# Attention of an eight-core transformer layer: half the row-sum matmuls, one VectorE addition instead, and the block's closing step placed inside the next block

## The chip, the cores and the metric

The kernel runs on all 8 cores of one Trainium2 chip (trn2). The cores form two dies (cores 0 to 3 and 4 to 7). The metric is the device time of one execution in microseconds (us), taken on the slowest core. Every core runs the same program on its own data; the cores exchange nothing.

## What is computed

One layer on x of shape (2, 4096, 4096) in float32. The core of the reference:

```python
xn = _layernorm(x, axis=-1)
x = x + attn(xn, w_qkv, w_o) + ffn(xn, gate, kernel, bias, lora_A, lora_B, ...)

# attn
qkv = einsum('bsd,od->bso', xn, w_qkv)      # 32 query heads, 8 key/value heads of 128
q, k = rope(q), rope(k)
scores = einsum('bhqd,bhkd->bhqk', q, k) / sqrt(128), causal mask
out = einsum('bhqk,bhkd->bhqd', softmax(scores), v)
return einsum('bso,do->bsd', out, w_o)

# ffn: one dense layer with bias and two low-rank terms
xn @ kernel + bias + B_eff (A_eff xn) + B_shared (A_shared xn)
```

Here batch is 2 and the sequence 4096, so four query heads share one key/value head, and each query position attends to itself and what is before it.

## The kernel before, in words

Each core owns 1024 of the 8192 tokens: two chunks of 512 (`CH`) of one batch, an early one (query block `qb` 0) and a late one (`qb` 1). It runs stages one after another, with a barrier between most: layer norm of the whole batch's 4096 tokens together with the K projection, the V projection (both `kp` on TensorE), the Q projection (`q_p`), the low-rank inputs (`lp_`), the attention (`a_`), the output projection (`w_p`), and the dense layer with the final sum (`f_p`). Weights and intermediate tensors (`sc_q`, `sc_k`, `sc_v`, `sc_xkv`) go through the chip's memory.

Nothing schedules the work but the code: `call` (L76) and `dma` (L103) append to one plan per engine, in the order in which the Python runs, and each engine executes its plan in that order. `wait` (L51) puts a wait on a semaphore in the plan of the engine that calls it; one counter per engine (`s_pe`, `s_ve`, `s_ac`) counts finished instructions. All TensorE matmuls that count up have the line L81, all others L86; all GpSimd loads have L111. `gd` is the GpSimd (POOL) queue, which issues the attention's loads.

The attention is `attention()` (L622). It runs over 8 key/value heads, 2 duos of query heads and 2 query blocks: 32 **blocks**, each for two heads `z` = 0 and 1. A block has 4 **visits** to chunks of 512 keys for `qb` 0 and 8 for `qb` 1 (`VISITS`, L26), 192 in all. The last visit of a block is the diagonal one (`DIAG`). A visit has two halves `g` of 256 keys, and a half has two key tiles `t` of 128. With two heads and two halves there are four probability tiles `a_p` (`psb`, index `2*z+g`).

`scores(z, g, ...)` (L663) makes two matmuls of K tile by Q into the two halves of `a_s`, one exponential of 128x1024 on ScalarE into `a_p`, and in the diagonal visit two products with the mask `p_cm` on VectorE. `avrows(z, g, ...)` (L693) makes, for each of the two key tiles, the value product (V tile by probabilities, into `a_av`) and the **row sum** (a weight of one column of ones, `p_onesb`, by the same probabilities, into the first partition of `a_rw`). These four matmuls alternate. They are accumulated in PSUM over the whole block.

The order within a visit is written out by hand (L744 to L756): scores of half 0 for both heads, `avrows` of half 1 of the visit before, scores of half 1, `avrows` of half 0. A score needs `a_s` of its head to be free (`scdep`, set by the exponential).

When the block's last `avrows` are done, the block is closed for each head (L761 to L782): the reciprocal of the row sum on VectorE (`a_rc`, 1x512), a matmul with a row of ones that spreads it over 128 partitions into `a_rw` (`p_onesf`; float32, it runs as two matmul instructions), a copy to `a_bc`, and the product of `a_av` and `a_bc` into `p_attn`. `a_rc`, `a_bc` and each head's Q tile exist once. The next block's loads (Q, then K and V of its first visit) are issued when the block's last reader is done (`qdep`, L727); K and V of the later visits go into three buffers each, one visit ahead (`load_kv`, L650).

After the attention the first output weights (`w_w`, 4 MB) are issued on the GpSimd queue (L786), and a barrier stands before the projection (L788).

## Time and profile before

| What | Value |
|---|---|
| Median of the runs before | 5046.68 us (2 runs: 4911.06 and 5182.3) |
| The profiled execution, its own time | 4911.6 us |
| Its span on the slowest core (core 6) | 4910.1 us |
| Spans of the 8 cores | 4871.8 to 4910.1 us, mean granted clock 0.901 to 0.905 |
| TensorE (PE) busy over the span | 4035.2 us, 82% |
| VectorE (DVE) busy | 1112.6 us, 23% |
| ScalarE (ACT) busy | 974.5 us, 20% |
| GpSimd (POOL) busy | 534.0 us, 11% |

The page is of one execution on its slowest core. PE is TensorE's matmuls, PEld its weight loads, which can overlap matmuls. Matmuls are pipelined: one is longer than the distance to the next, so the distance between the starts tells the rate. Where rows give the idle time before an instruction, the name behind the arrow is what ended it; "issue" is time in which the engine waited for nothing that the profile shows. PEclk is the TensorE clock that was granted, as a share of 2.4 GHz: 0.50 is the lower of the two levels, 1.2 GHz.

### The profile page before, as it was taken

Reading aid. Unit: us, or ns where it says so; the run is one execution under the profiler, and the core shown is the slowest. Engines: PE = TensorE matmul, PEld = TensorE weight load, DVE = VectorE, ACT = ScalarE, POOL = GpSimd, SP = SyncE. Lnnn points to the kernel's source line nnn. Section 1 sums busy time; section 2 is a strip of 40 time slices with the busy share of each in tenths; the row PEclk is TensorE's granted clock in tenths of the full one; section 3 lists DMA queues with packets and bytes.
Section 4 is the critical chain, followed back from the end, with each engine's and each line's share of the span. In section 5 each row is a group of like instructions: output and inputs, shape, how many; then the busy total and the mean of one; then the engine's idle time right before and its main releaser. Section 6 shows DMA issues by size and latency. Waiting matters only on the chain.

```text
span 4910.1 us, 44374 instructions; the slowest of 8 cores (4871.8 to 4910.1 us)
## 1 busy us (share of the span) xinstructions
PE 4035.2 (82%) x15827; PEld 1522.3 (31%) x16144; DVE 1112.6 (23%) x1874; ACT 974.5 (20%) x1041; POOL 534.0 (11%) x828
## 2 busy tenths in 40 slices
PE   3788786499939994888888888888888999568999
PEld 0333232144414441322222222222222444223334
DVE  0544454011002221122222222222222101012222
ACT  3112210000000000144444444444444000000000
POOL 1000000000000000122222222222221000000000
PEclk7899898799969997988988888888888999889999
DMA  9744622633156666011111111111113554466763
GB/s 139 140 95 86 117 79 63 131 99 111 54 113 90 102 87 133 19 36 35 35 33 37 32 33 36 34 35 35 33 36 62 101 106 88 98 140 138 143 135 97
DMA packets 398741, 394.61 MB, mean 80 GB/s; under 512 B 61888, under 2 KB 359104, under 8 KB 398400
## 3 DMA queue, kind: packets, MB, share of 16 engines
q0 software_dynamic: 214752, 223.94, 27.1%
q1 hardware_dynamic: 183776, 167.82, 11.4%
q8 instruction: 136, 2.23, 0.2%
q14 instruction: 77, 0.63, 0.0%
HBM read 470.30 MB, written 83.89 MB: 113 GB/s over the span
## 4 chain that ended last, share of the span: by engine, by line
PE 69%; DVE 10%; DMA 7%; another core or an unknown queue 7%; ACT 3%; issue 3%; SPq 0%; DVEq 0%; POOL 0%; ACTq 0%; POOLq 0%
PE kp L86 16%; PE a_rw L81 12%; PE w_p L86 9%; PE q_p L86 9%; PE a_av L86 8%; DMA f_at<-sc_at 5%; DVE a_rc L81 4%; PE a_s L86 4%; PE a_s L81 4%; PE f_p L86 4%; DVE f_s L81 2%; ACT a_p L81 1%; ACT lkv_q L81 1%; PE lp_pl L86 1%
## 5 line engine op out<-in xcount | busy, mean ns | idle before, releaser
L81 ACT ACTIVATE a_p<-a_s,p_btab 128x1024 bf16<-128x1024 f32 x768 | 814.0, 1111 | 2197.0 <-PE a_s L81 2197.0
L81 PE MATMUL a_rw<-a_p,p_onesb 128*1 128x512 bf16 x1536 | 581.4, 379 | 14.3 <-issue 7.7
L86 PE MATMUL a_av<-a_p,a_v 128*128 128x512 bf16 x1475 | 576.6, 391 | 0.0
L86 PE MATMUL f_p<-f_k,f_x 128*128 128x512 bf16 x2007 | 460.5, 385 | 126.8 <-DMA f_x<-sc_xkv 90.3
L86 PE MATMUL kp<-kv_w,kv_x 128*128 128x512 bf16 x1943 | 437.8, 380 | 92.0 <-DMA kv_w<-wvT 90.0
L86 PE MATMUL kp<-lkv_x,kv_w 128*128 128x512 bf16 x1985 | 462.9, 394 | 50.7 <-DVE kscr L81 21.9
L86 PE MATMUL q_p<-q_x,q_w 128*128 128x512 bf16 x1943 | 438.3, 381 | 78.9 <-DMA q_x<-sc_xkv 76.9
L86 PE MATMUL w_p<-w_w,p_attn 128*128 128x512 bf16 x1943 | 438.4, 381 | 4.3 <-SPq L182 2.3
L81 DVE TENSOR_TENSOR a_p<-a_p,p_cm 128x512 bf16<-128x512 bf16 x256 | 97.4, 422 | 1171.0 <-ACT a_p L81 1171.0
L81 PE MATMUL a_s<-a_q,a_k 128*128 128x512 bf16 x768 | 323.3, 421 | 16.4 <-DMA a_v<-sc_v 9.3
L86 PE MATMUL a_s<-a_q,a_k 128*128 128x512 bf16 x734 | 308.1, 420 | 14.1 <-ACT a_p L81 14.1
L81 PE MATMUL a_rw<-a_rc,p_onesf 1*128 1x512 f32 x128 | 124.4, 1070 | 236.7 <-DVE a_rc L81 236.7
L86 PEld LDWEIGHTS f_p<-f_k,f_x 128*128 128x128 bf16 x2048 | 198.1, 99 | 374.1 <-issue 154.2
L86 PEld LDWEIGHTS kp<-lkv_x,kv_w 128*128 128x128 bf16 x2032 | 204.1, 101 | 312.7 <-issue 100.3
L86 PEld LDWEIGHTS kp<-kv_w,kv_x 128*128 128x128 bf16 x1984 | 194.6, 98 | 325.8 <-issue 93.2
L86 PEld LDWEIGHTS q_p<-q_x,q_w 128*128 128x128 bf16 x1984 | 194.7, 98 | 313.2 <-issue 80.9
L111 POOL DMA_DIRECT2D a_k<-sc_k x384 | 200.8, 525 | 792.8 <-PE a_s L81 754.8
L86 PEld LDWEIGHTS w_p<-w_w,p_attn 128*128 128x128 bf16 x1984 | 194.7, 98 | 239.7 <-issue 7.4
L81 PEld LDWEIGHTS a_rw<-a_p,p_onesb 128*1 128x1 bf16 x1536 | 121.7, 79 | 428.3 <-issue 428.3
L86 PEld LDWEIGHTS a_av<-a_p,a_v 128*128 128x128 bf16 x1536 | 149.5, 97 | 318.3 <-issue 280.4
L81 ACT ACTIVATE lkv_q<-lkv_x 128x512 bf16<-128x512 bf16 x256 | 149.7, 623 | 485.1 <-PE lkv_pq L81 420.9
L81 DVE CAST kscr<-kp 128x512 bf16<-128x512 f32 x128 | 84.1, 688 | 693.7 <-PE kp L81 656.1
(90 smaller groups left out, 2085.1 us busy)
## 6 DMA issues: line engine op xcount, KB each, us to landing
lkv_x<-xTkv POOLq DMA_DIRECT2D x32, 1024.0 KB, 27.3
sc_xkv<-lkv_x SPq DMA_DIRECT2D x128, 256.0 KB, 4.0
kv_x<-sc_xkv SPq DMA_DIRECT2D x8, 4096.0 KB, 15.5
q_w<-wqT POOLq DMA_DIRECT2D x16, 2048.0 KB, 17.4
w_w<-woT POOLq DMA_DIRECT2D x8, 4096.0 KB, 26.5
f_k<-kern POOLq DMA_DIRECT2D x8, 4096.0 KB, 32.6
a_k<-sc_k POOLq DMA_DIRECT2D x384, 64.0 KB, 2.1
a_v<-sc_v POOLq DMA_DIRECT2D x192, 128.0 KB, 2.8
```

Source lines behind the costliest of these rows:

```text
L81: getattr(eng, m)(*aa, **kk).then_inc(s, st)
L86: getattr(eng, m)(*aa, **kk)
L111: eng.dma_start(**kk).then_inc(s, 16)
```

## The change

Three things change, all in `attention()`.

- In `scores`, VectorE adds the two key tiles of the probabilities (after the mask, where there is one) into a new bf16 tile `prow` (`a_w`, four of them), and `avrows` makes one row-sum matmul from it instead of two from `a_p`. The two value products now come first, then the row sum, which waits for the addition.
- The loops over heads, duos, query blocks and visits become one list of 192 visits (`sched`). K and V of a block's first visit are loaded during the visit before, the Q tiles are doubled (`qpar`) and loaded then too (`load_q`), and the three K and V buffers turn with the running number of the visit.
- The closing of a block (`finalize`) is placed in the next block's first visit, after its four scores and ahead of its first value products; the last `avrows` of the old block stand between the new block's first two and second two scores. `a_rc` and `a_bc` exist once per head.

```diff
             psb = [p2(nc.sbuf_tensor(f"a_p{i}", [128, 2 * CH], BF16)) for i in range(4)]
-            rcs = p2(nc.sbuf_tensor("a_rc", [1, CH], F32))
-            bcs = p2(nc.sbuf_tensor("a_bc", [128, CH], F32))
+            prow = [p2(nc.sbuf_tensor(f"a_w{i}", [128, CH], BF16)) for i in range(4)]
+            rcs = [p2(nc.sbuf_tensor(f"a_rc{i}", [1, CH], F32)) for i in range(2)]
+            bcs = [p2(nc.sbuf_tensor(f"a_bc{i}", [128, CH], F32)) for i in range(2)]
...
+            def load_q(bi):
+                kvh, duo, qb = blocks[bi]
+                qpar = bi % 2
+                qh = (4 * kvh + 2 * duo, 4 * kvh + 2 * duo + 1)
+                for z in range(2):
+                    h = qh[z]
+                    gd.wait(s_pe, qdep.get((z, qpar), 0))
+                    qld[(z, qpar)] = [
+                        gd.dma(out=qsb[z][0:64, qpar * CH:(qpar + 1) * CH],
...
                     exv[(z, g)] = mv
                     exk[(z, g)] = "ve"
+                    ve.wait(s_ve, mv)
                 else:
                     exv[(z, g)] = a
                     exk[(z, g)] = "ac"
+                    ve.wait(s_ac, a)
+                ve.wait(s_pe, prdep[zz])
+                pav = ve.call("tensor_add", prow[zz][:],
+                              psb[zz][:, 0:CH], psb[zz][:, CH:2 * CH])
+                exv[(z, g, "row")] = pav
...
                             psb[zz][:, t * CH:(t + 1) * CH],
                             start=(first and t == 0), stop=(last and t == 1),
                             inc=False)
-                    pe.call("matmul", p_rw[z][0:1, :], sb_onesb[:, 0:1],
-                            psb[zz][:, t * CH:(t + 1) * CH],
-                            start=(first and t == 0), stop=(last and t == 1))
+                pe.wait(s_ve, exv[(z, g, "row")])
+                pe.call("matmul", p_rw[z][0:1, :], sb_onesb[:, 0:1],
+                        prow[zz][:], start=first, stop=last)
                 pbdep[zz] = pe.ctr.v
...
+            load_q(0)
+            kvst[0] = load_kv(blocks[0][0], VISITS[sched[0][2]][1], 0)
+            for gi, (bi, vi, v) in enumerate(sched):
+                qpar = bi % 2
+                par = gi % 3
+                kl, vl = kvst[gi]
+                if gi + 1 < NG:
+                    nbi, nvi, nv_ = sched[gi + 1]
+                    kvst[gi + 1] = load_kv(blocks[nbi][0], VISITS[nv_][1],
+                                           (gi + 1) % 3)
+                    if nvi == 0:
+                        load_q(nbi)
+                scores(0, 0, v, par, qpar, kl)
+                scores(1, 0, v, par, qpar, kl)
+                if gi > 0:
+                    pvl = kvst[gi - 1][1]
+                    ppar = (gi - 1) % 3
+                    avrows(0, 1, ppar, pvl, False, vi == 0)
+                    avrows(1, 1, ppar, pvl, False, vi == 0)
+                scores(0, 1, v, par, qpar, kl)
+                scores(1, 1, v, par, qpar, kl)
+                if vi == 0 and bi > 0:
+                    finalize(bi - 1)
+                avrows(0, 0, par, vl, vi == 0, False)
+                avrows(1, 0, par, vl, vi == 0, False)
```

`finalize(bi)` holds the closing step of before, word for word but for the indices of `a_rc` and `a_bc`.

TensorE, one half visit inside a block, before. In the names, a_s is the scores, a_q and a_k the Q and K tiles, a_p the probabilities (0 and 1 are head 0, 2 and 3 head 1), a_v the V tile; the number behind a_s, a_av and a_rw is the head.

```order
L86 MATMUL a_s0<-a_q0,a_k1 128x512
L81 MATMUL a_s0<-a_q0,a_k1 128x512
L86 MATMUL a_s1<-a_q1,a_k1 128x512
L81 MATMUL a_s1<-a_q1,a_k1 128x512
L86 MATMUL a_av0<-a_p0,a_v1 128x512
L81 MATMUL a_rw0<-a_p0,p_onesb 1x512
L86 MATMUL a_av0<-a_p0,a_v1 128x512
L81 MATMUL a_rw0<-a_p0,p_onesb 1x512
L86 MATMUL a_av1<-a_p2,a_v1 128x512
L81 MATMUL a_rw1<-a_p2,p_onesb 1x512
L86 MATMUL a_av1<-a_p2,a_v1 128x512
L81 MATMUL a_rw1<-a_p2,p_onesb 1x512
```

The same half of a visit after the change (of the visit that uses the third K and V buffers); a_w is the sum of the two key tiles of a_p.

```order
L86 MATMUL a_s0<-a_q0,a_k2 128x512
L81 MATMUL a_s0<-a_q0,a_k2 128x512
L86 MATMUL a_s1<-a_q1,a_k2 128x512
L81 MATMUL a_s1<-a_q1,a_k2 128x512
L86 MATMUL a_av0<-a_p0,a_v2 128x512 x2
L81 MATMUL a_rw0<-a_w0,p_onesb 1x512
L86 MATMUL a_av1<-a_p2,a_v2 128x512 x2
L81 MATMUL a_rw1<-a_w2,p_onesb 1x512
```

Two of the four row sums are gone, and the value products of one head stand next to each other.

TensorE at the end of a block, before: the last `avrows`, the two broadcasts (a_rw from a_rc), and the next block's scores.

```order
L86 MATMUL a_av1<-a_p3,a_v0 128x512
L81 MATMUL a_rw1<-a_p3,p_onesb 1x512
L86 MATMUL a_av1<-a_p3,a_v0 128x512
L81 MATMUL a_rw1<-a_p3,p_onesb 1x512
L81 MATMUL a_rw0<-a_rc,p_onesf 128x512
L81 MATMUL a_rw1<-a_rc,p_onesf 128x512
L86 MATMUL a_s0<-a_q0,a_k0 128x512
L81 MATMUL a_s0<-a_q0,a_k0 128x512
L86 MATMUL a_s1<-a_q1,a_k0 128x512
L81 MATMUL a_s1<-a_q1,a_k0 128x512
L86 MATMUL a_s0<-a_q0,a_k0 128x512
```

The same place after.

```order
L86 MATMUL a_av0<-a_p1,a_v0 128x512 x2
L81 MATMUL a_rw0<-a_w1,p_onesb 1x512
L86 MATMUL a_av1<-a_p3,a_v0 128x512 x2
L81 MATMUL a_rw1<-a_w3,p_onesb 1x512
L86 MATMUL a_s0<-a_q0,a_k1 128x512
L81 MATMUL a_s0<-a_q0,a_k1 128x512
L86 MATMUL a_s1<-a_q1,a_k1 128x512
L81 MATMUL a_s1<-a_q1,a_k1 128x512
L81 MATMUL a_rw0<-a_rc0,p_onesf 128x512
L81 MATMUL a_rw1<-a_rc1,p_onesf 128x512
L86 MATMUL a_av0<-a_p0,a_v1 128x512 x2
L81 MATMUL a_rw0<-a_w0,p_onesb 1x512
```

The two broadcasts moved behind the four score pairs of the next block's first visit; the new block's value products stand behind them.

VectorE at the end of a block, before: mask products of the diagonal visit, the closing of heads 0 and 1, then the next block's first mask product.

```order
L81 TENSOR_TENSOR a_p1<-a_p1,p_cm4 128x512 x2
L81 TENSOR_TENSOR a_p3<-a_p3,p_cm4 128x512 x2
L81 RECIPROCAL a_rc<-a_rw0 1x512
L81 COPY a_bc<-a_rw0 128x512
L81 TENSOR_TENSOR p_attn<-a_av0,a_bc 128x512
L81 RECIPROCAL a_rc<-a_rw1 1x512
L81 COPY a_bc<-a_rw1 128x512
L81 TENSOR_TENSOR p_attn<-a_av1,a_bc 128x512
L81 TENSOR_TENSOR a_p0<-a_p0,p_cm4 128x512 x2
```

And after: the last addition of the diagonal visit (behind its mask product), the four additions of the new block's first visit, then the closing.

```order
L81 TENSOR_TENSOR a_w3<-a_p3 128x512
L81 TENSOR_TENSOR a_w0<-a_p0 128x512
L81 TENSOR_TENSOR a_w2<-a_p2 128x512
L81 TENSOR_TENSOR a_w1<-a_p1 128x512
L81 TENSOR_TENSOR a_w3<-a_p3 128x512
L81 RECIPROCAL a_rc0<-a_rw0 1x512
L81 COPY a_bc0<-a_rw0 128x512
L81 TENSOR_TENSOR p_attn<-a_av0,a_bc0 128x512
L81 RECIPROCAL a_rc1<-a_rw1 1x512
L81 COPY a_bc1<-a_rw1 128x512
L81 TENSOR_TENSOR p_attn<-a_av1,a_bc1 128x512
L81 TENSOR_TENSOR a_w0<-a_p0 128x512
```

The first reciprocal moved behind the additions for all four exponentials of the new block's first visit.

## Rows read from the trace of the kernel before

**Rows 1.** Busy time by stretch (times each), PEclk, DMA share, GB/s; core 6.

```profile
core 6: us, PE busy (x) PEld busy (x) DVE busy (x) ACT busy (x) POOL busy (x), PEclk, DMA share, GB/s
2053.00:3800.00 1747.00, 1472.39 (x4641) 422.50 (x4734) 397.09 (x448) 813.96 (x768) 409.76 (x694) 0.88 0.13 36
...
3840.00:4200.00 360.00, 358.26 (x1636) 163.23 (x1668) 35.97 (x52) 0.00 (x0) 10.05 (x6) 1.00 0.49 90
```

**Rows 2.** Chain that ended last, within 2053 to 3800 us, by line.

```profile
by line: PE a_rw L81 32.6%; PE a_av L86 23.5%; DVE a_rc L81 12.1%; PE a_s L86 12.0%; PE a_s L81 10.3%; ACT a_p L81 3.6%; issue 3.0%; DVE a_bc L81 1.3%; DVE p_attn L81 1.3%; DVEq L60 0.2%; ACTq L60 0.0%; PE w_p L86 0.0%; SPq L60 0.0%; SPq L1
```

**Rows 3.** Timeline, one half visit: start, length (us), engine, line, instruction, [idle before].

```profile
2613.05 0.39 PE L86 MATMUL a_s<-a_q,a_k 128*128 128x512 bf16 x1
2613.28 0.38 PE L81 MATMUL a_s<-a_q,a_k 128*128 128x512 bf16 x1
...
2613.76 2.12 ACT L81 ACTIVATE a_p<-a_s,p_btab 128x1024 bf16<-128x1024 f32 x2 [1.26 <-PE a_s L81]
2613.93 0.38 PE L86 MATMUL a_av<-a_p,a_v 128*128 128x512 bf16 x1
2614.23 0.08 PEld L81 LDWEIGHTS a_rw<-a_p,p_onesb 128*1 128x1 bf16 x1 [0.42 <-issue]
2614.24 0.38 PE L81 MATMUL a_rw<-a_p,p_onesb 128*1 128x512 bf16 x1
...
2614.55 0.39 PE L86 MATMUL a_av<-a_p,a_v 128*128 128x512 bf16 x1
...
2616.43 0.39 PE L86 MATMUL a_s<-a_q,a_k 128*128 128x512 bf16 x1
```

**Rows 4.** Timeline at the end of a block (2624 to 2642 us).

```profile
2624.62 3.35 DVE L81 RECIPROCAL a_rc<-a_rw 1x512 f32<-1x512 f32 x1 [1.13 <-PE a_rw L81]
...
2625.40 0.38 PE L81 MATMUL a_rw<-a_p,p_onesb 128*1 128x512 bf16 x1
...
2628.12 2.04 PE L81 MATMUL a_rw<-a_rc,p_onesf 1*128 1x512 f32 x2 [2.34 <-DVE a_rc L81]
...
2630.33 0.69 DVE L81 COPY a_bc<-a_rw 128x512 f32<-128x512 f32 x1 [2.36 <-PE a_rw L81]
...
2631.13 0.69 DVE L81 TENSOR_TENSOR p_attn<-a_av,a_bc 128x512 bf16<-128x512 f32 x1
...
2631.74 3.33 DVE L81 RECIPROCAL a_rc<-a_rw 1x512 f32<-1x512 f32 x1
...
2635.22 2.04 PE L81 MATMUL a_rw<-a_rc,p_onesf 1*128 1x512 f32 x2 [5.06 <-DVE a_rc L81]
2637.19 0.61 PE L86 MATMUL a_s<-a_q,a_k 128*128 128x512 bf16 x1
...
2637.59 0.63 PE L81 MATMUL a_s<-a_q,a_k 128*128 128x512 bf16 x1
2638.01 0.63 PE L86 MATMUL a_s<-a_q,a_k 128*128 128x512 bf16 x1
...
2638.32 2.12 ACT L81 ACTIVATE a_p<-a_s,p_btab 128x1024 bf16<-128x1024 f32 x2 [15.68 <-PE a_s L81]
...
2639.58 0.58 PE L86 MATMUL a_s<-a_q,a_k 128*128 128x512 bf16 x1 [0.50 <-ACT a_p L81]
...
2641.78 0.38 PE L81 MATMUL a_rw<-a_p,p_onesb 128*1 128x512 bf16 x1
```

**Rows 5.** Chain of waits, two of head 0's reciprocals: start, length, what.

```profile
2583.45 3.36 DVE a_rc L81
...
2692.73 3.36 DVE a_rc L81
```

**Rows 6.** Busy time by stretch, at a block end.

```profile
2587.00:2600.00 13.00, 7.44 (x12) 1.75 (x13) 6.02 (x5) 2.61 (x3) 4.66 (x8) 0.50 0.22 64
```

**Rows 7.** Groups of the page: busy us, mean ns, idle before.

```profile
L81 PE MATMUL a_rw<-a_p,p_onesb 128*1 128x512 bf16 x1536 | 581.4, 379 | 14.3 <-issue 7.7
L81 DVE TENSOR_TENSOR a_p<-a_p,p_cm 128x512 bf16<-128x512 bf16 x256 | 97.4, 422 | 1171.0 <-ACT a_p L81 1171.0
```

**Rows 8.** Timeline, the diagonal visit's exponentials and mask products.

```profile
2617.14 2.12 ACT L81 ACTIVATE a_p<-a_s,p_btab 128x1024 bf16<-128x1024 f32 x2 [1.26 <-PE a_s L81]
...
2618.35 0.76 DVE L81 TENSOR_TENSOR a_p<-a_p,p_cm 128x512 bf16<-128x512 bf16 x2 [20.61 <-ACT a_p L81]
```

**Rows 9.** Timeline, the first output weights and projection; landing time from the page's DMA issues.

```profile
w_w<-woT POOLq DMA_DIRECT2D x8, 4096.0 KB, 26.5
...
3770.95 1.72 POOL L111 DMA_DIRECT2D w_w<-woT  x1 [1.78 <-issue]
...
3799.93 2.29 PE L86 MATMUL w_p<-w_w,p_attn 128*128 128x512 bf16 x5 [2.29 <-SPq L182]
```

More of the change, by code:

```diff
@@ L627, in attention @@
                 ve.waitd(cmld)
-                qsb = [p2(nc.sbuf_tensor(f"a_q{i}", [128, CH], BF16)) for i in range(2)]
+                qsb = [p2(nc.sbuf_tensor(f"a_q{i}", [128, 2 * CH], BF16)) for i in range(2)]
                 kb = [p2(nc.sbuf_tensor(f"a_k{i}", [128, CH], BF16)) for i in range(3)]
@@ L636, in attention @@
                 p_rw = [p2(nc.psum_tensor(f"a_rw{i}", [128, CH], F32)) for i in range(2)]
-                qdep = [0, 0]
+                blocks = [(kvh, duo, qb)
+                          for kvh in range(KVH) for duo in range(2) for qb in range(2)]
+                sched = []
+                for bi, (kvh, duo, qb) in enumerate(blocks):
+                    vis = [v for v in range(12) if VISITS[v][0] == qb]
+                    for vi, v in enumerate(vis):
+                        sched.append((bi, vi, v))
+                NG = len(sched)
+                qdep = {}
+                qld = {}
                 kdep = [0, 0, 0]
@@ L642, in attention @@
                 pbdep = [0, 0, 0, 0]
+                prdep = [0, 0, 0, 0]
                 exv = {}
@@ L646, in attention @@
                 rwdep = [0, 0]
-                rcs_dep = 0
-                bcs_dep = 0
+                rcsd = [0, 0]
+                bcsd = [0, 0]
+                kvst = {}
                 def load_kv(kvh, pos, par):
@@ L670, in scores @@
                                 kb[par][:, (2 * g + t) * 128:(2 * g + t + 1) * 128],
-                                qsb[z][:], start=True, stop=True, inc=(t == 1))
+                                qsb[z][:, qpar * CH:(qpar + 1) * CH],
+                                start=True, stop=True, inc=(t == 1))
                     spv = pe.ctr.v
+                    qdep[(z, qpar)] = spv
                     ac.wait(s_pe, spv)
@@ new lines, in finalize @@
+                def finalize(bi):
+                    kvh, duo, qb = blocks[bi]
+                    qh = (4 * kvh + 2 * duo, 4 * kvh + 2 * duo + 1)
+                    for z in range(2):
+                        h = qh[z]
+                        ve.wait(s_pe, pbdep[2 * z])
+                        ve.wait(s_pe, pbdep[2 * z + 1])
+                        ve.wait(s_pe, rcsd[z])
+                        rv = ve.call("reciprocal", rcs[z][0:1, :], p_rw[z][0:1, :])
+                        rwdep[z] = rv
+                        pe.wait(s_ve, rv)
+                        bv = pe.call("matmul", p_rw[z][:, :], sb_onesf[0:1, :],
+                                     rcs[z][0:1, :], start=True, stop=True)
+                        rcsd[z] = bv
+                        ve.wait(s_pe, bv)
+                        ve.wait(s_ve, bcsd[z])
+                        cv = ve.call("tensor_copy", bcs[z][:], p_rw[z][:, :])
+                        rwdep[z] = cv
+                        ve.wait(s_ve, cv)
+                        nv2 = ve.call("tensor_mul",
+                                      sb_attn[:, h * TOWN + qb * CH:
+                                              h * TOWN + (qb + 1) * CH],
+                                      p_av[z][:], bcs[z][:])
+                        avdep[z] = nv2
+                        bcsd[z] = nv2
@@ L784, in build_program @@
+                gl = NG - 1
+                avrows(0, 1, gl % 3, kvst[gl][1], False, True)
+                avrows(1, 1, gl % 3, kvst[gl][1], False, True)
+                finalize(len(blocks) - 1)
         attention()
```

78 lines of the change are left out of this document (10 added, 68 removed).

## The prediction

> **What bounds the kernel now.** I first took the two wide stretches that have the attention's matmul shapes and the output projection's [rows 1]. In the attention (2053 to 3800 us) TensorE is busy for 1472 of 1747 us, ScalarE for 814, VectorE for 397 and GpSimd for 410, at a mean granted clock of 0.88; in the projection the clock is 1.00, and 1636 matmuls take 358 us, 0.22 us each. So the attention belongs to TensorE, and what it loses there it loses to something other than a busy neighbour. The chain of waits inside the attention says to what [rows 2]: TensorE's row sums (a_rw) hold 32.6% of it, the value products (a_av) 23.5%, the scores (a_s) 22.3%, and VectorE's reciprocal (a_rc) 12.1%. Those are two different things, a stream of matmuls and a stall at block ends, so I read one of each in the timeline.
>
> The stream [rows 3]: four score matmuls start 0.22 us apart (the first value product starts 0.88 after the first of them); from there value products and row sums alternate, 0.31 us apart (2613.93, 2614.24, 2614.55). Eight of these and the four scores are half a visit, 2613.05 to 2616.43: 3.38 us, of which ScalarE's two exponentials take 2.12. The row sum's weight load (one column) starts only as its own matmul does, not under the matmul before. The score pairs write alternate halves of a tile as well and still start 0.22 apart, so what costs 0.09 is, as I read it, the switch between 128-column and 1-column weights.
>
> The block end [rows 4]: the last row sum starts at 2625.40, the next block's first score at 2637.19. Between them lies one chain, for each head: reciprocal 3.35, broadcast matmul pair 2.04, copy 0.69, product 0.69; head 1's reciprocal waits in VectorE's queue for all of head 0's. From the first reciprocal's start (2624.62) to the first score it is 12.57 us. The same reciprocal of the next long and short blocks together comes at 2583.45 and 2692.73 [rows 5]: 109.28 us for 24 half visits, which by 3.38 are 81.1; 28.2 are left, **14.1 us lost per block end**. Of those 11.5 are the gap and the rest the restart at half clock: the granted clock is 0.50 from 2587 to 2600 [rows 6], scores start 0.43 apart, and head 0's next pair waits for its exponential until 2639.58; row sums are back at 0.31 from 2641.78, 6.6 us after the second broadcast began [rows 4]. Check: 16 such pairs of blocks are 1748 us, the length of the attention.
>
> **The change, part by part.** (1) Row sums. There are 1536 of them, 379 ns long each [rows 7]; half go. Each pair of value products now runs back to back and one row sum follows. Value product to value product I cost at 0.22, the pitch of equal-width neighbours in [rows 1, 3]; then 0.31 and 0.31 for the two switches: 0.84 where there were 1.25. A half visit becomes 0.88 + 2 x 0.84 = **2.56 us**, 0.82 less; 192 visits have 384 halves: **-315 us**. The unseen pitch lies between 0.22 and 0.31; at 0.31 a half visit is 2.74 and the part brings 246. Below: 330, if rounding is in our favour.
>
> The Trainium skill (TensorE: Matmul & The Clock Gate, Step-by-step: what each phase is for) says that the array's queue pulls the next weights ahead of the running matmul, so that neighbours are spaced by the moving columns alone. By that, a removed row sum is worth 0.22, not 0.41. The trace agrees for equal widths and contradicts it where widths alternate.
>
> (2) Does something else end later than 2.56? ScalarE: the exponentials start 0.71 after the first score, the second ends at 2.83, and a score that waits for one starts 0.15 after its end (2638.32 + 1.11 to 2639.58) [rows 3, 4]: head 1's next score may go at 2.98 and is due at 2.56 + 0.44 = 3.00. It just fits; there is no more to gain from TensorE here without ScalarE becoming the bound. VectorE: 768 new additions of 128x512 bf16. The nearest row is the mask product, 0.38 us apart and 0.42 long, started 0.10 after its exponential [rows 8]; ends are 0.38 and the 0.69 of the PSUM copy [rows 4]. They are off the path: in a plain half visit head 1's sum is ready at 2.83 + 0.10 + 0.42 = 3.35, and its row sum is due at 2.56 + 0.88 + 0.84 + 0.44 = 4.72. In the diagonal visit VectorE has 2 x (0.76 + 0.42) plus gaps, 2.5 of 2.56 us, and is ready at about 4.5; it fits. At 0.69 each it would be 0.4 late in 64 half visits, +25 us. The added waits sit in VectorE's queue, behind which only the next sums stand.
>
> (3) Loads. The new block's first K, V and Q are issued a visit ahead, not after the last row sum. This removes nothing: TensorE waited for the reciprocals, not for them. 0 us; GpSimd's work does not grow.
>
> (4) Block end. This is where the text of the change and the order part. The four first exponentials of the next block are done before the stall, but TensorE still takes its instructions in order: after the scores of half visit 0 and 1 stand both broadcasts, so it waits for **both reciprocals** before any value product. And VectorE reaches the first reciprocal only after the additions for those last scores. Let T be the start of the new block's third score pair. Exponentials end at T+2.83, addition at +2.93, reciprocal at +3.31; the chain of 12.57 is unchanged, so the first value product starts at T+15.88. TensorE's own work ended at T+0.88: **15.0 us of gap against 11.5**. The restart: the second broadcast begins at T+13.91, so full clock by the same 6.6 us at T+20.5. Head 0's three matmuls run at half clock (0.5 lost), head 1's value product waits for its accumulator's last reader (13.91 + 2.21 + 0.80 + 0.69 + 0.10 = T+17.7, 0.45 lost), then 2.8 us at half clock lose 1.4. Together 17.4, **3.3 more than 14.1**; 31 block ends of 32 move (the last stays): **+102 us**. Ends: 16.4 (no wait, prompt clock) is +71; 19 is +152.
>
> (5) After the attention. The first output weights are issued at 3770.95 and land 26.5 later; the projection starts at 3799.93 [rows 9]. Five half visits less 0.82 bring the end 4.1 closer: 24.9 are left, so about 2 us show. Bounds 0 and 5.
>
> Sum against the profiled execution (4911.6 us, its span 4910.1 on the slowest core): 4911.6 - 315 + 102 + 2 = **4701 us**, -4.3%. The median before is 5046.68, of two runs at 4911.06 and 5182.3; the profile goes with the lower, and so does my forecast. 
>
> **Rivals.**
> - *A row sum is worth only its columns* (0.22, case W): the switch costs nothing by itself and another cause keeps the 0.31 for the rest. 384 x 2 x 0.22 = 169; 4911.6 - 169 + 104 = 4847. For it: no row shows two value products in a row. Against: scores at 0.22.
> - *The block end is hidden, as the new order suggests* (case H): if TensorE did not stand still, 14.1 would fall to about 4 (broadcasts): 4911.6 - 315 + 2 - 31 x 10.1 = 4286. Against: the broadcasts stand in line ahead of the value products, and nothing after them can pass.
> - *The clock thins* (case P): were the denser stream granted 0.81 instead of 1.00, each of ten matmuls would cost 0.05 more, 384 x 0.5 = 192: 4893. Against: the projection, denser still, has 1.00 [rows 1]. The Trainium skill (same page, Seeing it yourself) has a peak-current limit of 13/16 when three cores of a die run dense matmuls; this trace, with eight, does not show it.
> - *The clock does not come back* (case C, the slow side): after a gap of 15 us, cut by two broadcasts, the clock stays at its lower level well into the block. A half visit at the low level costs 10 x 0.21 = 2.1 us more. The gain of 211 is gone at 100 such half visits; through all short blocks (some 107 beyond the restart) it is 4926; slower by over 2% from 147 on; in the whole stage 5421. For it: the stage has 0.88 now. Against: it comes back 6.6 us after the broadcast, at every block end I read, and no stall is left inside a block.
>
> **How the numbers follow.** Forecast 0.81, W 0.10, P 0.03, H 0.02, C 0.04 (three quarters of it slower by over 2%). The likeliest's own ends: low 4911.6 - 330 + 71 = 4653; high 4911.6 - 246 + 152 + 25 + 5 = 4848 with all of it bad together. W ends there too. I take 4640 to 4840; what lies above is most of P and C, below is H. Faster by over 2% (under 4813): the forecast, H and the lower edge of W, 0.84. Within 2%: the rest of W, P, a quarter of C, 0.13. Slower: 0.03.
>
> **What would show it.** Timeline: half visits 2.5 to 2.6 us apart, with value product to value product at 0.22 (if 0.31, part 1 is wrong by 70 us). Row sums 768 in number. From the last score of a new block's first visit to its first value product 15 us, with the first reciprocal starting 3.3 us after the third score pair; TensorE's waits for a_rc 31 x (5.8 + 5.1) and the last pair, some 345 us in all (237 now: 64 x 3.7). Consecutive same-head reciprocals of a long and a short block: 24 x 2.56 + 2 x 17.4 = 96.2 us apart in place of 109.3. Attention near 1535 us long. If that distance is under 85, the block end was hidden; if TensorE's idle before a_av names VectorE in mid-block, the additions are late; a granted clock under 0.8 in the stretch speaks for C.

## The result, and the profile after

The changed kernel takes 4713.77 us (median of 11 runs, lowest 4697.02); against the kernel before the ratio is 0.9579, with a 95% interval of 0.9554 to 0.9603: 4.2% faster. The chip has executions in which a die runs at a lower clock, before and after alike; the ratio is of the undisturbed ones, and the kernel before has a median of 5139.74 with them and of about 4914 without. The profiled execution has a span of 4713.8 us on the slowest core, core 3.

The forecast was 4701 against a profiled execution of 4911.6, a ratio of 0.957. As a share of that execution it came out; the parts don't all hold, and the places are named further down. To compare stages across runs I use the length of the attention, from the start of the first exponential to the start of the last product into p_attn: 1745.6 us before (2053.0 to 3798.6), 1527.9 after (2049.4 to 3577.3).

The stretch of the attention after the change, columns as in [rows 1]:

```profile
core 3: us, PE busy (x) PEld busy (x) DVE busy (x) ACT busy (x) POOL busy (x), PEclk, DMA share, GB/s
...
2515.00:2529.00 14.00, 3.68 (x4) 0.99 (x4) 8.74 (x6) 1.33 (x2) 0.99 (x2) 0.55 0.06 19
...
2534.00:2552.00 18.00, 17.92 (x71) 5.11 (x69) 8.80 (x22) 14.79 (x15) 7.76 (x14) 1.00 0.21 61
2049.00:3577.00 1528.00, 1172.77 (x3967) 320.78 (x3965) 711.83 (x1215) 813.99 (x768) 410.56 (x696) 0.83 0.15 41
```

TensorE has 300 us less work, ScalarE and GpSimd have the same, VectorE 315 more. Within a block TensorE is as full as before (17.92 of 18 us; 17.85 of 18 before, from 2600 to 2618); what grew is the share of time at the block ends, so the mean granted clock fell from 0.88 to 0.83.

One half visit, from the timeline; it answers to [rows 3]:

```profile
2503.18 0.39 PE L86 MATMUL a_s<-a_q,a_k 128*128 128x512 bf16 x1
...
2503.88 2.12 ACT L81 ACTIVATE a_p<-a_s,p_btab 128x1024 bf16<-128x1024 f32 x2 [0.43 <-PE a_s L81]
2504.05 0.59 PE L86 MATMUL a_av<-a_p,a_v 128*128 128x512 bf16 x2
2504.58 0.38 PE L81 MATMUL a_rw<-a_w,p_onesb 128*1 128x512 bf16 x1
2504.89 0.60 PE L86 MATMUL a_av<-a_p,a_v 128*128 128x512 bf16 x2
2505.16 0.42 DVE L81 TENSOR_TENSOR a_w<-a_p 128x512 bf16<-128x512 bf16 x1 [1.12 <-ACT a_p L81]
...
2505.73 0.39 PE L86 MATMUL a_s<-a_q,a_k 128*128 128x512 bf16 x1
```

2503.18 to 2505.73 are 2.55 us in place of 3.38. Two value products in a row are 0.59 long together, so their starts are 0.22 apart; where the widths change, starts are still 0.31 apart.

A block end, answering to [rows 4]; T, the start of the new block's third score pair, is 2513.51:

```profile
2513.51 0.39 PE L86 MATMUL a_s<-a_q,a_k 128*128 128x512 bf16 x1
...
2514.17 0.38 PE L81 MATMUL a_s<-a_q,a_k 128*128 128x512 bf16 x1
...
2516.51 0.42 DVE L81 TENSOR_TENSOR a_w<-a_p 128x512 bf16<-128x512 bf16 x1 [0.58 <-ACT a_p L81]
2516.85 3.34 DVE L81 RECIPROCAL a_rc<-a_rw 1x512 f32<-1x512 f32 x1
2520.33 2.04 PE L81 MATMUL a_rw<-a_rc,p_onesf 1*128 1x512 f32 x2 [5.78 <-DVE a_rc L81]
...
2523.88 3.33 DVE L81 RECIPROCAL a_rc<-a_rw 1x512 f32<-1x512 f32 x1
2527.36 2.04 PE L81 MATMUL a_rw<-a_rc,p_onesf 1*128 1x512 f32 x2 [4.99 <-DVE a_rc L81]
2529.34 1.03 PE L86 MATMUL a_av<-a_p,a_v 128*128 128x512 bf16 x2
...
2531.14 1.01 PE L86 MATMUL a_av<-a_p,a_v 128*128 128x512 bf16 x2 [0.26 <-DVE p_attn L81]
```

The reader sees the reciprocal right behind the last addition (T+3.34), the value product at T+15.83, and the gap, 2514.39 to 2529.34, of 15.0 us. The same reciprocal of a long and a short block together comes at:

```profile
2267.69 3.27 DVE a_rc L81
...
2363.44 3.27 DVE a_rc L81
```

95.75 us for what took 109.28 [rows 5]; 24 half visits are 61.3, so a block end loses 17.2. TensorE's longest waits in 2040 to 3600 us (who waited for whom: us, times, longest):

```profile
PE a_rw L81 <- DVE a_rc L81: 342.6, 64, 5.8
...
PE w_p L86 <- DMA w_w<-woT: 12.3, 1, 12.3
...
PE a_av L86 <- DVE p_attn L81: 8.0, 31, 0.3
```

No addition (a_w) is among them. Two are new: 0.3 us at each block end for head 0's or head 1's product, which the prediction had in its sum, and 12.3 us for the projection's first weights, where [rows 9] had only the barrier.

What stands behind the attention grew too. From the start of the last product into p_attn to the end of the span it is 1111.5 us before and 1136.5 after, on the slowest core of each: 10.1 more until the projection starts, 6.1 more of waiting for the dense layer's first input (before, then after), and 10.1 more in the dense layer itself (569.9 and 580.0 us), less 1.2 in the projection. The mean over the eight cores is 14.5 more, 9.1 of it in the dense layer.

```profile
PE f_p L86 <- DMA f_x<-sc_xkv: 90.3, 1, 90.3
PE f_p L86 <- DMA f_x<-sc_xkv: 96.4, 1, 96.4
```

### The profile page after: what moved, and what is told of

Read it like the earlier page. It is cut to its first block, busy times and chain, and to the rows that moved or that the text cites. A ratio compares the mean times of both kernels' runs of the same rounds, so it can differ in the third digit from the quotient of the medians.

```text
span 4713.8 us, 46036 instructions; the slowest of 8 cores (4661.6 to 4713.8 us)
## 1 busy us (share of the span) xinstructions
PE 3745.1 (79%) x15376; PEld 1419.8 (30%) x15376; DVE 1427.8 (30%) x2642; ACT 974.0 (21%) x1041; POOL 534.3 (11%) x828
## 4 chain that ended last, share of the span: by engine, by line
PE 70%; DVE 10%; DMA 8%; another core or an unknown queue 7%; ACT 3%; issue 2%; SPq 0%; DVEq 0%; POOL 0%; ACTq 0%; POOLq 0%
PE kp L86 19%; PE q_p L86 9%; PE w_p L86 9%; PE a_av L86 8%; PE a_rw L81 7%; PE f_p L86 5%; DMA f_at<-sc_at 5%; PE a_s L86 4%; DVE a_rc L81 4%; PE a_s L81 3%; DVE f_s L81 1%; DMA lkv_x<-xTkv 1%; ACT lkv_q L81 1%; PE lp_pl L86 1%
## 5 line engine op out<-in xcount | busy, mean ns | idle before, releaser
L86 PE MATMUL f_p<-f_k,f_x 128*128 128x512 bf16 x2048 | 471.1, 390 | 133.0 <-DMA f_x<-sc_xkv 96.4
L81 DVE TENSOR_TENSOR a_w<-a_p 128x512 bf16<-128x512 bf16 x768 | 326.5, 425 | 638.8 <-ACT a_p L81 561.0
L86 PE MATMUL kp<-kv_w,kv_x 128*128 128x512 bf16 x1984 | 440.7, 380 | 89.9 <-DMA kv_w<-wvT 89.9
L86 PE MATMUL q_p<-q_x,q_w 128*128 128x512 bf16 x1984 | 440.9, 380 | 80.9 <-DMA q_x<-sc_xkv 80.9
L86 PE MATMUL kp<-lkv_x,kv_w 128*128 128x512 bf16 x2032 | 461.9, 391 | 47.1 <-DVE lkv_x L81 25.2
L86 PE MATMUL a_av<-a_p,a_v 128*128 128x512 bf16 x1536 | 487.2, 400 | 8.5 <-DVE p_attn L81 8.0
L86 PE MATMUL w_p<-w_w,p_attn 128*128 128x512 bf16 x1984 | 440.1, 380 | 12.3 <-DMA w_w<-woT 12.3
L81 PE MATMUL a_rw<-a_rc,p_onesf 1*128 1x512 f32 x128 | 130.4, 1119 | 342.6 <-DVE a_rc L81 342.6
L86 PEld LDWEIGHTS f_p<-f_k,f_x 128*128 128x128 bf16 x2048 | 199.7, 100 | 388.7 <-issue 172.4
L86 PE MATMUL a_s<-a_q,a_k 128*128 128x512 bf16 x768 | 304.6, 397 | 13.4 <-DMA a_k<-sc_k 9.9
L81 PE MATMUL a_rw<-a_w,p_onesb 128*1 128x512 bf16 x768 | 302.6, 394 | 0.0
L81 PE MATMUL a_s<-a_q,a_k 128*128 128x512 bf16 x768 | 299.5, 390 | 0.0
L86 PEld LDWEIGHTS kp<-lkv_x,kv_w 128*128 128x128 bf16 x2032 | 202.7, 100 | 309.6 <-issue 85.9
L86 PEld LDWEIGHTS kp<-kv_w,kv_x 128*128 128x128 bf16 x1984 | 194.5, 98 | 325.7 <-issue 93.1
L86 PEld LDWEIGHTS q_p<-q_x,q_w 128*128 128x128 bf16 x1984 | 194.6, 98 | 317.0 <-issue 84.4
L86 PEld LDWEIGHTS w_p<-w_w,p_attn 128*128 128x128 bf16 x1984 | 194.4, 98 | 248.8 <-issue 15.8
L81 DVE RECIPROCAL a_rc<-a_rw 1x512 f32<-1x512 f32 x64 | 213.6, 3337 | 0.0
L81 DVE TENSOR_TENSOR f_s<-f_p,f_at 128x512 f32<-128x512 f32 x64 | 44.3, 692 | 531.9 <-DMA f_at<-sc_at 317.7
```

The lines of the kernel that those rows point to most:

```text
L81: getattr(eng, m)(*aa, **kk).then_inc(s, st)
L86: getattr(eng, m)(*aa, **kk)
```

## Experiments: the parts alone

**Closing back at its old place.** The row sums, additions and early loads of the change stay:

```diff
-                    if gi > 0:
+                    if vi > 0:
...
-                    if vi == 0 and bi > 0:
-                        finalize(bi - 1)
                     avrows(0, 0, par, vl, vi == 0, False)
                     avrows(1, 0, par, vl, vi == 0, False)
+                    if gi + 1 == NG or sched[gi + 1][1] == 0:
+                        avrows(0, 1, par, vl, False, True)
+                        avrows(1, 1, par, vl, False, True)
+                        finalize(bi)
```

> The changed kernel with one part undone: a block is closed behind its own last row sums again, before the next block's scores; additions, halved row sums and early loads stay. Theory (the rows bring all, the new place of the closing costs 3.3 us at each of 31 block ends): 4911.6 - 315 + 2 = 4599, about 0.936 of the kernel before and 110 less than the changed kernel; half visits 2.56, gap at the block end 11.5 us. Rival (the new place or the overlap of scores and closing brings part of the gain): at or above the changed kernel's 4714.

Measured: lowest 4625.94, ratio 0.9386 (0.9331 to 0.9440) to the kernel before; attention 1447.7 us (2041.6 to 3489.3), **80 less than with the whole change**. TensorE's wait for the reciprocals is 252.4 us, not 342.6. So the new place costs, as expected (ratio 0.9386, where 0.936 was worked out; in us it lies 27 above the 4599, 17 of them in the attention); the size is 2.6 us per block end and not 3.3, because the old place also lost something when visits got shorter. From this run's timeline, the last value products of a block:

```profile
2332.05 0.59 PE L86 MATMUL a_av<-a_p,a_v 128*128 128x512 bf16 x2 [0.20 <-DVE a_p L81]
...
2333.44 0.59 PE L86 MATMUL a_av<-a_p,a_v 128*128 128x512 bf16 x2 [0.41 <-DVE a_p L81]
```

Without the next block's scores between them, the diagonal visit's products wait for the mask (0.2 and 0.4 us), which the change hides.

**Only the row sums**, in the kernel before, with its loads:

```diff
+                    ve.wait(s_pe, prdep[zz])
+                    pav = ve.call("tensor_add", prow[zz][:],
+                                  psb[zz][:, 0:CH], psb[zz][:, CH:2 * CH])
+                    exv[(z, g, "row")] = pav
...
+                    pe.wait(s_ve, exv[(z, g, "row")])
+                    pe.call("matmul", p_rw[z][0:1, :], sb_onesb[:, 0:1],
+                            prow[zz][:], start=first, stop=last)
```

> The kernel before with only the row sums changed (addition on VectorE, one row sum for two); loads and closing as before. Theory (early loads bring nothing): 4599 like the run before it, within 15 us. Rival (the loads at a block's start were hidden only by luck, and with shorter visits they end last): 20 us and more above it, with TensorE waiting for a_k or a_v at block starts.

Measured: lowest 4631.75, ratio 0.9400 (0.9324 to 0.9477); attention 1447.9 us (2049.0 to 3496.9) against 1447.7 with early loads. The early loads bring nothing here. The time is not within 15 us of 4599, as expected, but like the run before it, within 6 us.

**Only the closing's place and the loads**, row sums as before:

```diff
-                    pav = ve.call("tensor_add", prow[zz][:],
-                                  psb[zz][:, 0:CH], psb[zz][:, CH:2 * CH])
...
-                    pe.call("matmul", p_rw[z][0:1, :], sb_onesb[:, 0:1],
-                            prow[zz][:], start=first, stop=last)
+                        pe.call("matmul", p_rw[z][0:1, :], sb_onesb[:, 0:1],
+                                psb[zz][:, t * CH:(t + 1) * CH],
+                                start=(first and t == 0), stop=(last and t == 1))
```

> The changed kernel with its row sums undone: two from the probabilities, no additions; the closing and the loads stay at their new places. Half visits 3.38. Without additions in VectorE's queue the first reciprocal starts 1.2 us before the new block's third score pair, so the gap is 10.5 and not 15.0 us and a block end loses 12.9 in place of 14.1: 4911.6 - 31 x 1.2 = 4875. Rival (the new place costs by itself, through the scores that stand ahead of it or a later clock): 4911.6 + 102 = 5014.

Measured: lowest 4849.55, ratio 0.9842 (0.9766 to 0.9918); attention 1667.7 us (2053.2 to 3720.9), 78 less than before. The direction is the theory's: **alone, the new place is a gain, if one of under 2%; it is a loss together with the additions**. The gain is twice what I expected. The timeline of a block end of this run says why:

```profile
2394.51 0.38 PE L81 MATMUL a_rw<-a_p,p_onesb 128*1 128x512 bf16 x1
...
2394.99 3.35 DVE L81 RECIPROCAL a_rc<-a_rw 1x512 f32<-1x512 f32 x1 [1.99 <-PE a_rw L81]
...
2398.49 1.09 PE L81 MATMUL a_rw<-a_rc,p_onesf 1*128 1x512 f32 x2 [1.37 <-DVE a_rc L81]
...
2404.57 2.04 PE L81 MATMUL a_rw<-a_rc,p_onesf 1*128 1x512 f32 x2 [4.99 <-DVE a_rc L81]
2406.55 0.61 PE L86 MATMUL a_av<-a_p,a_v 128*128 128x512 bf16 x1
```

The first broadcast comes while the clock is still up (granted 1.00 from 2395 to 2399, 0.53 in the ten us behind) and takes 1.09 us, not 2.04; the gap is 9.6 us, not 10.5. So it is at 31 of 32 block ends (1.09 to 1.15). In the kernel before, on its slowest core, 7 of 32 had it at the upper clock already, so some 24 x 0.95 = 23 us come on top of the 37. The other 18 were not traced to a cause; part of them is in the restart, which varies: here matmuls are at full pace from 2409.7 on, 5.1 us after the second broadcast began, over all block ends 6.5 in the mean, and 6.9 in the kernel before.

**One reciprocal ahead of the additions**, the whole change otherwise:

```diff
                         avrows(1, 1, ppar, pvl, False, vi == 0)
+                    if vi == 0 and bi > 0:
+                        recip0()
                     scores(0, 1, v, par, qpar, kl)
```

> The changed kernel with one instruction per block end moved on VectorE: head 0's reciprocal stands ahead of the additions for the new block's third and fourth exponential, not behind them. Theory: it starts at T+0.8 and not T+3.3 (T: start of the third score pair), everything behind it 2.5 us earlier, 31 x 2.5 = 79: 4635. Rival (TensorE's place in the row, not VectorE's queue, sets the gap): no change, 4714.

Measured: lowest 4607.07, ratio 0.9349 (0.9298 to 0.9400); attention 1424.1 us (2054.1 to 3478.2), 104 less than with the change; the time is 28 us under the 4635 expected, mostly by the clock, as follows. The timeline has the reciprocal at 2347.14, T+0.78 (T is 2346.36), the first broadcast again at the upper clock, and the gap at 11.5 us:

```profile
2345.20 0.38 PE L81 MATMUL a_rw<-a_w,p_onesb 128*1 128x512 bf16 x1
...
2347.14 3.34 DVE L81 RECIPROCAL a_rc<-a_rw 1x512 f32<-1x512 f32 x1
...
2350.63 1.09 PE L81 MATMUL a_rw<-a_rc,p_onesf 1*128 1x512 f32 x2 [3.23 <-DVE a_rc L81]
...
2358.68 1.03 PE L86 MATMUL a_av<-a_p,a_v 128*128 128x512 bf16 x2
```

The rival, that TensorE's place in the row alone sets the gap, falls: nothing was changed on TensorE. 2.56 us per block end come from the queue, 79 in all; 0.95 come from the broadcast's clock, at 19 block ends of 32 (at 11 it takes 2.04 us here too), some 18. That is 97 of the 104.

This is not yet all that VectorE's queue costs. Head 0's last row sum starts at 2345.20, and in the kernel with the closing alone the reciprocal started 0.48 us after that row sum (2394.51 to 2394.99). Here it starts 1.94 after it, because the addition for the new block's second exponential still stands ahead of it. By these rows, 1.46 us are left per block end, an estimate of 45 us that no run took back.

## Experiments: what a half visit is bound by

**Both heads' value products first**: two switches of width instead of four.

```diff
+                def avpair(g, par, vl, first, last):
+                    for z in range(2):
...
+                        for t in range(2):
+                            kt = 2 * g + t
+                            pe.call("matmul", p_av[z][:],
...
+                    for z in range(2):
+                        zz = 2 * z + g
+                        pe.wait(s_ve, exv[(z, g, "row")])
+                        pe.call("matmul", p_rw[z][0:1, :], sb_onesb[:, 0:1],
+                                prow[zz][:], start=first, stop=last)
```

> The changed kernel with the four value products of both heads in a row, then both row sums: two switches of weight width in a half visit, not four. By switches alone TensorE would need 0.88 + 3 x 0.22 + 0.31 + 0.22 + 0.31 = 2.38 us. Theory (ScalarE's two exponentials and the way back to the score hold a half visit at 2.54): 2.54, 384 x 0.02, 4706. Rival (ScalarE has room): 2.38, 384 x 0.17 = 65 us less, 4649.

Measured: lowest 4699.94, ratio 0.9549 (0.9520 to 0.9578); attention 1526.8 us (2044.1 to 3570.9) against 1527.9. The total is as expected, but not for the reason that I gave. Half visits are not 2.54: inside a block they alternate between 2.36 and 2.52, 2.44 in the mean.

```profile
2476.74 0.39 PE L86 MATMUL a_s<-a_q,a_k 128*128 128x512 bf16 x1
...
2479.09 0.39 PE L86 MATMUL a_s<-a_q,a_k 128*128 128x512 bf16 x1
...
2479.70 0.38 PE L86 MATMUL a_s<-a_q,a_k 128*128 128x512 bf16 x1
...
2481.61 0.39 PE L86 MATMUL a_s<-a_q,a_k 128*128 128x512 bf16 x1
```

In the longer ones, head 1's scores start 0.61 behind head 0's and not 0.44; that is where ScalarE shows. The half visits gain some 30 us in all, and the block ends give them back: in the mean, the half visit that holds the closing takes 19.55 us in place of 19.11, and the one behind it 3.55 in place of 3.02, 31 x 0.97 = 30. TensorE's waits for the product into p_attn grew from 8.0 to 24.7 us, since head 1's value products now stand right behind head 0's.

**The same with half the exponential.** It leaves out the exponential of the second key tile of each half, whose probabilities stay zero.

```diff
-                    a = ac.call("activation", psb[zz][:], p_sc[z][:], AF.Exp,
+                    a = ac.call("activation", psb[zz][:, 0:CH], p_sc[z][:, 0:CH], AF.Exp,
```

> As the run before it, but the exponential covers only the first of the two key tiles; the second tile of the probabilities is zeroed once and stays so. ScalarE's part of a half visit falls by half. Theory of the switches: TensorE alone, 2.38 us a half visit, 65 us less than the changed kernel. If half visits stay near 2.55, the switch is not what costs (then value products or their waits do).

Measured: span 4654.7; attention 1470.3 us (2052.0 to 3522.3), 57.6 less. A half visit, from the timeline:

```profile
2430.25 0.39 PE L86 MATMUL a_s<-a_q,a_k 128*128 128x512 bf16 x1
...
2432.09 0.59 PE L81 MATMUL a_rw<-a_w,p_onesb 128*1 128x512 bf16 x2
...
2432.61 0.39 PE L86 MATMUL a_s<-a_q,a_k 128*128 128x512 bf16 x1
```

2.36 us, where 2.38 was worked out with 0.09 for each of two switches. So TensorE alone needs 2.36, and with whole exponentials the same order takes 2.44: ScalarE takes back 0.08 of the 0.19 that two switches fewer bring. The 2.55 of the changed kernel is TensorE's own stream of four switches; its waits name the exponential with 1.6 us in the whole stage.

## Experiments: a closing without broadcasts

**Ones 128 columns wide.** Each row sum stands in all partitions, so the broadcasts go. This is the kernel before otherwise.

```diff
+                onesw = p2(nc.sbuf_tensor("a_on", [128, 128], BF16))
+                onv = ve.call("memset", onesw[:], 1.0)
...
-                        pe.call("matmul", p_rw[z][0:1, :], sb_onesb[:, 0:1],
+                        pe.call("matmul", p_rw[z][:, :], onesw[:, :],
...
-                                rv = ve.call("reciprocal", rcs[0:1, :], p_rw[z][0:1, :])
+                                rv = ve.call("reciprocal", bcs[:], p_rw[z][:, :])
```

> The kernel before with the weight of ones 128 columns wide: each row sum then stands in all 128 partitions, so the two broadcasts of a block go and the reciprocal is taken of 128x512. No additions; 1536 row sums as before. Theory of the switches: all 12 matmuls of a half visit 0.22 apart, 2.60 us, 384 x 0.78 = 300 less; of the block end 2 x 2.0 for broadcasts and the new scores no longer stand behind the second reciprocal: value products wait for reciprocal and product of either head, about 8 us from the last row sum, 6 less, 190: 4912 - 490 = 4420. Rival (each row sum costs 0.31 whatever its width): half visits 3.38, 4912 - 190 = 4720.

Measured: median 4433.88, ratio 0.8996 (0.8970 to 0.9022); attention 1260.1 us (2042.0 to 3302.1), 485 less than before, with all 1536 row sums and no addition. The timeline of a half visit shows the widths alike and the pitch at 0.22 throughout, 2341.49 to 2344.08, 2.59 us:

```profile
2341.49 0.38 PE L86 MATMUL a_s<-a_q,a_k 128*128 128x512 bf16 x1
...
2342.35 0.38 PE L86 MATMUL a_av<-a_p,a_v 128*128 128x512 bf16 x1
2342.57 0.38 PE L81 MATMUL a_rw<-a_p,a_on 128*128 128x512 bf16 x1
...
2344.08 0.38 PE L86 MATMUL a_s<-a_q,a_k 128*128 128x512 bf16 x1
```

The rival (0.31 for any row sum) falls: the switch of width is what costs. And the waits name something that had been covered: `PE a_s L86 <- DMA a_k<-sc_k` 160.0 us in 31 times. That raised the question what early loads are worth now.

**Wide ones with early loads**: order and loads of the change, with the closing queued right behind the old block's last row sums and working straight from PSUM.

```diff
+                        rv = ve.call("reciprocal", bcs[z][:], p_rw[z][:, :])
+                        rwdep[z] = rv
+                        ve.wait(s_ve, rv)
+                        nv2 = ve.call("tensor_mul",
...
+                                      p_av[z][:], bcs[z][:])
```

> The kernel with wide ones and copies, but without the copies: reciprocal and product read PSUM, loads stay early. Theory: new value products wait for their head's product; 3.34 + 0.11 + 0.69 for head 0 and as much again for head 1, less the 0.87 of scores between: 5.8 us lost per block end, 31 x 5.3 = 165 more than with copies, attention about 1181 us. That is 80 less than with wide ones and late loads (1260), which is then what early loads are worth once the broadcasts are gone. Rival (early loads bring nothing here either): 1260.

Measured: lowest 4433.58, ratio 0.8989 (0.8935 to 0.9044); attention 1256.7 us (2038.5 to 3295.2). **A miss**: not 80 less, but 3. The 160 us for a_k are gone, and in their place are 170.5 us for the product:

```profile
2297.11 3.36 DVE L81 RECIPROCAL a_bc<-a_rw 128x512 f32<-128x512 f32 x1 [0.91 <-PE a_rw L81]
...
2301.41 0.38 PE L86 MATMUL a_av<-a_p,a_v 128*128 128x512 bf16 x1 [2.68 <-DVE p_attn L81]
...
2305.47 0.58 PE L86 MATMUL a_av<-a_p,a_v 128*128 128x512 bf16 x1 [2.69 <-DVE p_attn L81]
```

The wait per block end is as I worked it out (5.4 us, 5.8 expected). What I left out is the clock: between the two waits of 2.7 us it falls to 0.50, and matmuls start 0.43 apart until 2308.4. A wait moved from one cause to another of the same length; the loads run beside the reciprocals and are worth nothing on their own in this form either.

**Copies out of PSUM**: as the last, but VectorE first empties the accumulators.

```diff
+                    for z in range(2):
+                        ve.wait(s_pe, pbdep[2 * z])
+                        ve.wait(s_pe, pbdep[2 * z + 1])
+                        ve.wait(s_ve, clo[z])
+                        avdep[z] = ve.call("tensor_copy", avs[z][:], p_av[z][:])
+                        rwdep[z] = ve.call("tensor_copy", bcs[z][:], p_rw[z][:, :])
+                    for z in range(2):
...
+                        rv = ve.call("reciprocal", bcs[z][:], bcs[z][:])
```

> The order and loads of the changed kernel, no additions, a weight of ones 128 columns wide, and at a block's end VectorE first copies both accumulators of both heads out of PSUM (4 x 0.69 us), then takes reciprocals and products from the copies, behind nobody. Theory: half visits 2.60; a block end costs about 0.5 us of TensorE, and the clock stays at its upper level: attention 384 x 2.60 + 31 x 0.5 + 12 = 1026 us in place of 1748, 4190 in all. Rival (reciprocals of 3.3 us on VectorE hold the mask products or the next copies): TensorE waits for VectorE in mid-block, 4250 and more.

Measured: lowest 4186.63 (4920.37 for the kernel before on the same chip); attention 1016.2 us (2039.6 to 3055.8), where 1026 counts some 12 us behind it. **This is the version that beats both.** Its attention, and a block end in its timeline:

```profile
core 7: us, PE busy (x) PEld busy (x) DVE busy (x) ACT busy (x) POOL busy (x), PEclk, DMA share, GB/s
2040.00:3056.00 1016.00, 1001.61 (x4605) 445.88 (x4604) 429.50 (x512) 812.89 (x768) 409.96 (x694) 1.00 0.22 60
```

```profile
2314.41 0.38 PE L81 MATMUL a_rw<-a_p,a_on 128*128 128x512 bf16 x1
2314.62 0.38 PE L86 MATMUL a_s<-a_q,a_k 128*128 128x512 bf16 x1
2314.64 0.68 DVE L81 COPY a_bc<-a_rw 128x512 f32<-128x512 f32 x1
...
2316.13 0.38 PE L81 MATMUL a_rw<-a_p,a_on 128*128 128x512 bf16 x1
...
2316.43 3.34 DVE L81 RECIPROCAL a_bc<-a_bc 128x512 f32<-128x512 f32 x1
2316.66 0.38 PE L86 MATMUL a_av<-a_p,a_v 128*128 128x512 bf16 x1
```

TensorE stands still for 0.3 us, not 15, the same reciprocals run beside the next block, and the clock is 1.00 from end to end.

## Experiments: the projection's first weights

**The second weights held back** until the first have landed, in the changed kernel:

```diff
                         gd.wait(s_pe, wdep[ni])
+                        if dc == 0:
+                            gd.waitd(gv0)
```

> The changed kernel; only the second output weights (4 MB) are not issued until the first have landed. In the changed kernel the projection waits 12.3 us for the first, which took 35 us to land and not 26.5, the second having been issued 25.6 us after them. Theory (the two share the transfer engines): the first land about 27 us after their issue, the wait falls to about 4 us. Rival (the other cores' traffic or the end of the attention slows it): it still lands after 35 us and the wait stays at 12.

Measured: the first weights, issued at 3549.47, land after 29.9 us instead of 35.2, and the wait falls from 12.3 to 7.1 (span 4705.1). That is 5.2 of the some 8 us that I expected. But it compares the slowest core of one run with that of another, and the other cores say less: with the change, the first weights land after 24.3 to 35.2 us on the eight cores, 30.2 in the middle (23.9 to 28.5 in the kernel before), and with the second held back after 24.9 to 30.6, 29.3 in the middle. The 35.2 is one core's; that the second transfer slows the first is at most 1 us on a typical core and 5 on that one. Why they take some 30 us and not 26.5 stays open.

**The weights in pieces** during the last visits, in the kernel with copies:

```diff
+                    if NG - 18 <= gi < NG - 2:
+                        load_w((gi - NG + 18) // 8, (gi - NG + 18) % 8)
```

> The kernel with wide ones and copies; the first two output weights are issued in 16 pieces of 512 KB, one in each of 16 of the attention's last visits, not as a whole at its end. Theory: the projection's wait of 22.6 us goes, K and V still arrive in time (a piece takes 3.4 us of a visit's 5.2): 4186 - 22 = 4164. Rival (pieces delay K and V in the same queue): TensorE waits for a_k in the last 18 visits, no gain.

Measured: lowest 4185.82, against 4186.63: no gain that can be told. The wait for weights is gone, but the barrier's is now 10.3, and the attention is 1022.9 us (2034.7 to 3057.6), 6.7 longer: K loads land after a median of 4.0 us in its last visits, 2.1 without the pieces. Of 22.6 us at most 12 had been to gain, the rest lay beside the last closing, and half went to K.

## Why the prediction was right, and where not

- *What bounds it*: right: TensorE's stream and the closing chain. But they are not independent. Alone, the row sums bring 1745.6 - 1447.9 = 298 us and the closing's place 78; together they bring 218 and not 376. The additions stand in VectorE's queue ahead of the reciprocal: one reciprocal moved ahead gives back 104 of the 158, and by the rows some 45 more lie in the addition still ahead of it. The sum of the prediction saw this, as its term (4).
- *(1) Row sums, 315 us*: right. The half visit is 2.55 (2.56); the pitch that no row showed is 0.22. 384 x 0.83 = 319 less 16 for the mask wait, plus small change, is the 298. That the switch of widths costs 0.09 was an inference from neighbours; the wide ones show it, at 0.22 with both widths alike. Rival W falls.
- *(2) ScalarE just fits*: right for 2.55, which TensorE's stream sets. That there is no more to gain without ScalarE was too strong: fewer switches bring the half visit to 2.44, half the exponential to 2.36. The additions are late nowhere in the changed kernel.
- *(3) Loads, 0 us*: right, 1447.7 against 1447.9. With wide ones they take the place of another wait of the same length.
- *(4) Block end, 17.4*: 17.2 in the trace; gap 15.0 as worked out. The cause is shown: one reciprocal moved ahead of two additions gives back 104 us. The term +102 measured 80 against the same row sums at the old place, where a block end costs 14.6 and not 14.1: I took the old loss as a constant, though shorter visits expose the mask there. Together with the row sums' 298 for 315 this is some luck: in the attention, 17 us too much gain and 22 too much loss nearly cancel, and -213 was worked out where -218 was measured. Rival H falls, C and P too: full clock from 2533.7, 6.4 us after the second broadcast, and 1.00 within blocks.
- *(5) After the attention, 2 us, bounds 0 and 5*: **wrong in size**, the one mis-sized term that shows in the total: what follows the last product grew by **25 us** (1111.5 to 1136.5), and the total came out at -196 where -211 was worked out (the attention 5 better, the stages ahead of it 4 shorter, this term 23 worse). The projection starts 11.4 us after the last product, 1.3 before; +10. I took the landing time of 26.5 us as fixed and only moved its end; the first weights take 35.2 on this core. On the other seven cores the projection starts 1.3 to 7.2 us after the last product. The 6 us in front of the dense layer and the 10 in it had no term at all, as if stages that the change doesn't touch kept their length. Their cause stays open; the granted clock in the dense layer, mean of eight cores, is 0.965 after and 0.976 before.
- *The step that failed*, next to term (5), is the base of the sum, 4911.6: **"the profile goes with the lower, and so does my forecast"**. 4701 is a forecast of the lower of two runs. Against the median that was given, 5046.68, it reads as 6.8% faster, and against the ten runs' median of 5139.74 as 8.5%; 4.2% was measured. What the change gives is a share: 0.957 of 5046.68 would be 4830, at the upper edge of my range, and of 5139.74 it is 4919, outside. Of the ten runs before, three lie at 4911 to 4925 and seven at 5093 to 5286; of the eleven after, eight lie at 4697 to 4724. The two runs that I had lay 271 us apart, more than the whole effect, and I gave one number on one base without saying what the other base makes of it. The range, too, took in the costs of the change alone and nothing of this spread.

## What to carry to other kernels

Before an in-order engine is given a wait, read two queues: what stands behind the wait on its engine, and what stands ahead of the releasing instruction on the other; here a reciprocal that was ready but queued behind two additions, which waited for their exponentials, cost 104 us in a whole kernel. Two changes that meet in one queue are not to be added up from runs of each alone (298 and 78 gave 218). To take a chain off the path, free its inputs with a copy instead of moving the chain: four copies of 0.69 us per block were worth 240 us in the attention (1256.7 to 1016.2). A small stationary matrix may be worth widening: with as many columns as its neighbours it costs less, and its result arrives where it is needed.

## What the runs showed that I had not expected

- A stall has a second price through the clock, and its length alone doesn't tell it. A float32 broadcast pair takes 1.09 us at the upper clock and 2.04 at the lower. After waits of 5 us and more (4.99 to 5.8) it was 2.04 at every block end in each kernel; after 1.4 us it was 1.09 to 1.15 at all 31. Between, it can be either: 2.04 at 24 of 32 after 2.3 us (kernel before), but 1.09 at 24 of 32 after 2.9 us (closing back at its old place) and at 19 after 3.2 us. Two waits of 2.7 us with four matmuls between them ended at the lower clock as well. In the kernel before there is an order in time: the first broadcast takes 1.40, 1.17 and 1.21 us at the first three block ends, 1.09 at the next four, 1.96 at the eighth, and 2.04 at all 24 behind it. The other cores of the same run, with the same kernel, go nearly the same way, but change at another block end: 9 to 28 of 32 are at 2.04. So neither the wait's length nor the kernel settles it; what does was not tested.
- A reciprocal of 128x512 takes 3.34 to 3.36 us like one of 1x512: the 127 other partitions cost it nothing, so broadcasting the row sum ahead of it costs nothing on VectorE.
- A wait that goes can uncover one of the same length: 160.0 us for K became 170.5 us for the product, and the kernel stayed at 4434.
